# Moving a reciprocal, weight copies, biases and an attention-output projection within the seventh attention step, and interleaving the last four output tiles

## The reference

```python
x = _layernorm(x + _L0_attn_ref(x, w_qkv, b_qkv, w_out, b_out))
x = _layernorm(x + _L0_ffn_ref(x, up_weight, down_weight, up_scale, down_scale, output_scale))
# attn: softmax(q k^T / sqrt(32) + causal) v, then @ w_out.T + b_out
# ffn:  relu((x @ sign(up).T) * up_scale) @ sign(down).T * down_scale * output_scale
```

## Time and profile before

| what | value |
|---|---|
| median of 3 runs | 760.01 us (758.69 to 762.78) |
| the profiled execution | 762.44 us |
| its span in the trace | 760.7 us |
| PE busy | 717.5 us (94%) |
| PEld, DVE, POOL, ACT busy | 68%, 55%, 52%, 43% |
| mean granted TensorE clock | 0.983 of full speed |

### The profile page before, as it was taken

The page is one execution under the profiler, slowest core; times in us unless marked ns, Lnnn a source line. Parts: engine busy times, 40 slices in busy tenths (PEclk is TensorE's granted clock), DMA queues, the critical chain, the costliest instruction groups (busy, mean ns, idle before and its releaser), DMA issues.

```text
span 760.7 us, 11957 instructions
## 1 busy us (share of the span) xinstructions
PE 717.5 (94%) x4112; PEld 515.3 (68%) x4112; DVE 419.7 (55%) x1024; ACT 324.3 (43%) x647; POOL 392.1 (52%) x527
## 2 busy tenths in 40 slices
PE   6899999999999999999798889999999999999993
PEld 4688666666676666665453657678888787878882
DVE  4176485674857657476378441384683359324515
ACT  5211365665655566555345386532321222222210
POOL 4561467493864839657259328662352235223333
PEclk9999999999999999999889999999999999999997
DMA  6975464636455362563727364515005001000101
GB/s 235 297 214 168 103 186 135 177 83 176 147 155 162 93 176 88 155 181 99 188 90 235 97 211 142 164 44 153 16 15 152 28 1 56 1 1 14 43 0 56
DMA packets 47797, 90.02 MB, mean 118 GB/s; under 512 B 5821, under 2 KB 14781, under 8 KB 47609
## 3 DMA queue, kind: packets, MB, share of 16 engines
q1 hardware_dynamic: 38712, 84.02, 37.2%
q10 hardware_dynamic: 9024, 5.24, 2.3%
HBM read 59.38 MB, written 29.61 MB: 117 GB/s over the span
## 4 chain that ended last, share of the span: by engine, by line
PE 79%; DVE 6%; POOL 5%; issue 4%; DMA 4%; ACT 2%; SPq 1%; DVEq 0%; POOLq 0%; ACTq 0%
PE ps_proj L1096 10%; PE ps_heads L1197 8%; PE ps_proj L1248 7%; PE ps_unit L1248 6%; PE ps_score L1273 6%; PE ps_unit L1132 6%; PE ps_unit L1219 5%; PE ps_unit L1164 5%; PE ps_sum L1191 4%; PE ps_score L1164 4%; PE ps_score L1132 3%; PE ps_sum L1273 2%; PE ps_heads L1273 2%; PE ps_unit L1273 2%; PE ps_score L1116 1%
## 5 line engine op out<-in xcount | busy, mean ns | idle before, releaser
L780 POOL TENSOR_TENSOR hid_low<-hid_raw,hid_high 128x512 fp32r<-128x512 f32 (+1 forms) x80 | 90.0, 1126 | 168.2 <-DVE hid_high L1031 167.0
L837 ACT ACTIVATE probs<-ps_unit 128x512 f32<-128x512 f32 (+3 forms) x214 | 101.8, 490 | 88.8 <-PE ps_unit L1164 84.5
L837 ACT ACTIVATE probs<-ps_score 128x512 f32<-128x512 f32 (+3 forms) x170 | 82.4, 495 | 80.0 <-PE ps_score L1164 77.0
L743 POOL TENSOR_SCALAR_AFFINE_SELECT probs<-probs 128x128 f32<-128x128 f32 x256 | 75.9, 315 | 73.5 <-ACT probs L837 70.0
L943 DVE CUSTOM_DVE_ANT_0 ps_unit<-ps_unit,causal 128x128 f32<-128x128 f32 (+3 forms) x162 | 80.6, 513 | 48.4 <-PE ps_unit L1132 47.5
L1031 DVE CAST hid_high<-hid_raw 128x512 fp32r<-128x512 f32 (+1 forms) x80 | 34.1, 426 | 126.9 <-ACT hid_raw L900 126.3
L1132 PE MATMUL ps_unit<-stack 96*128 96x512 f32 (+3 forms) x242 | 84.4, 360 | 8.5 <-DVE maxes L943 5.5
L756 POOL TENSOR_TENSOR added<-added,probs 128x512 f32<-128x512 f32 x64 | 82.4, 1298 | 0.0
L1197 PE MATMUL ps_heads<-probs,v_rows 128*32 128x512 f32 (+3 forms) x768 | 81.0, 504 | 0.0
L1164 PE MATMUL ps_unit<-stack 98*128 98x512 f32 (+2 forms) x214 | 77.0, 363 | 0.1
L737 POOL TENSOR_TENSOR parts<-qk_full,parts 128x512 fp32r<-128x512 f32 x32 | 41.3, 1290 | 56.7 <-ACT parts L816 56.7
(11 more groups left out here) (216 smaller groups left out, 1469.9 us busy)
## 6 DMA issues: line engine op xcount, KB each, us to landing
stack<-qk_parts SPq DMA_DIRECT2D x96, 256.0 KB, 4.6
qk_parts<-parts SPq DMA_DIRECT2D x32, 512.0 KB, 2.9
v_all<-h_even ACTq DMA_DIRECT2D x16, 256.0 KB, 3.6
v_rows<-v_all SPq DMA_DIRECT2D x8, 512.0 KB, 4.2
heads_t<-heads_sb SPq DMA_DIRECT2D x16, 256.0 KB, 2.6
x_tile<-x_rows SPq DMA_DIRECT2D x16, 256.0 KB, 5.3
raw<-up_w SPq DMA_DIRECT2D x8, 512.0 KB, 3.6
raw<-down_w SPq DMA_DIRECT2D x8, 512.0 KB, 3.6
```

What stands on the lines that cost most here:

```text
L743: nc.gpsimd.affine_select(out=tile, in_=tile, compare_op=ALU.is_ge, fill=0.0, base=0, pattern=[[1, P]], channel_multiplier=-1).then_inc(s_ ...
L780: nc.gpsimd.tensor_tensor(parts2[1][:, (HM * s + n) % 3, 0:tokens(s)], full[:, n % 2, 0:tokens(s)], parts2[0][:, (HM * s + n) % 3, 0:token ...
L837: nc.scalar.activation(probs[:, (NP * s + n) % RING, 0:width], bank(what, s, n)[:, off:off + width], ACT.Exp, scale=SCALE).then_inc(s_exp, 1)
```

## The change

It alters slot numbers in `plan()` and adds one wait on DVE. Nothing is computed that was not computed before.

```diff
-ALONE = [[11.2, 13.5, 15.7, 18.3, 28, 30, 32.2, 36, 39.5, 43, 46.5, 50.3],
+ALONE = [[11.2, 13.5, 15.7, 18.3, 28, 30, 32.2, 36, 40.6, 43.3, 46.5, 50.3],
...
-        put(t + (43.9 if paired else 39.4 - s % 2), "sum_added", s)
+        put(t + (43.9 if paired else (40.5, 38.4)[s % 2]), "sum_added", s)
...
-    signs = [late + 39, late + 41.5] + [late + 44 + 3.3 * k for k in range(14)] + [late + 88.9, late + 91.6]
+    signs = [late + 37.2, late + 39.4] + [late + 44 + 3.3 * k for k in range(14)] + [late + 88.9, late + 91.6]
...
-        put(at + (2.9, 5, 3)[k], "invert", k)
-        put(at + (4.4, 6, 4)[k], "scatter", k)
+        put(at + (6.9, 5, 3)[k], "invert", k)
+        put(at + (8.5, 6, 4)[k], "scatter", k)
...
-        put(late + 40 + 1.3 * i, "bias", 0, i)
+        put(late + 44.5 + 1.5 * i, "bias", 0, i)
         for m in range(12):
-            put((late + 45, late + 47.6, last + 1.7, last + 4.5)[i] + 0.22 * m, "attn", 0, 12 * i + m)
-        put((late + 47.5, last + 2.3, last + 4.6, last + 7.4)[i], "y", 0, i)
+            put((late + 45.6, late + 48.2, last + 2.4, last + 5)[i] + 0.22 * m, "attn", 0, 12 * i + m)
+        put((late + 48.1, last + 2.9, last + 5.1, last + 7.8)[i], "y", 0, i)
...
-        put((last + 12.2, last + 12.7, last + 14, last + 14.5)[i], "turn", 0, i)
+        put((last + 13.2, last + 13.7, last + 14.8, last + 15.3)[i], "turn", 0, i)
...
-            put(t + m if r else last + 14.8 + 1.95 * m, "up", r, m)
+            put(t + m if r else last + 15.6 + 1.95 * m, "up", r, m)
             if r < len(ROUNDS) - 1 or m < HM - 2:
-                put(t + m + 2.5 if r else last + 19.7 + 1.95 * m, "down", r, m)
+                put(t + m + 2.5 if r else last + 20.5 + 1.95 * m, "down", r, m)
...
         for q in tiles:
-            put(end, "z", i, q)
-            put(end + 1.05 + q, "ln2", i, q)
-            put(end + 1.95 + q, "out", i, q)
+            if r < len(ROUNDS) - 1:
+                put(end, "z", i, q)
+                put(end + 1.05 + q, "ln2", i, q)
+                put(end + 1.95 + q, "out", i, q)
+            else:
+                put(end + (0, 0.1, 0.2, 1.1)[q], "z", i, q)
+                put(end + 1 + q, "ln2", i, q)
+                put(end + (2.5, 3.5, 4.5, 5.5)[q], "out", i, q)
...
                 for m in range(12):
-                    put(t + (5.2 if i else 3) + at, "attn", i + 1, 12 * q + m)
-                put(t + (6 if i else 4.2) + at, "y", i + 1, q)
-                put(t + (6.7 if i else 5.1) + at, "ln1", i + 1, q)
-                put(t + (7.4 if i else 6.4) + at, "turn", i + 1, q)
+                    put(t + (5.2 if i else 4) + at, "attn", i + 1, 12 * q + m)
+                put(t + (6 if i else 5.2) + at, "y", i + 1, q)
+                put(t + (6.7 if i else 6.1) + at, "ln1", i + 1, q)
+                put(t + 7.4 + at, "turn", i + 1, q)
...
                     dve.wait_ge(s_zr, TT * s + n + 1)
+                    wait(dve, s_mom2, TT * s + n)
                     nc.vector.bn_stats(stats[:, 1, :], z_sb[:, n, :]).then_inc(s_bn, 1)
```

## The result

The changed kernel takes 752.33 us (median of 4 runs, 750.92 to 753.71), the one before 760.25 beside it: a ratio of 0.990, 95% interval 0.987 to 0.993, so some 7.9 us or 1.0% are gained where 15.1 were forecast. The profiled execution took 753.71 us, with a span of 751.6; against the 760.7 of before that is 9.1 us less. The times of the two profiled executions, 762.44 and 753.71, lie 2.2 and 1.4 us above their medians, so that part of the difference to 7.9 is between executions and not between kernels.

A forecast was written before the change was run, and what follows sets the result against it. PE was taken to set the pace, with the gain in its waits and half clock from 360 to 450 us. Terms -8.5 - 4.5 - 1.0 + 0.2 - 1.3 = -15.1 us gave 745 us, range 741.5 to 751.

The forecast's parts named there:

- The first reciprocal: Seventh step, DVE: reciprocal moved behind eight maxima removes PE's 4.4 us wait and 4.7 us of half clock; -8.5 us.
- The rival of late sums: Gathered sums land 2 us later, DVE and PE stand again, the clock falls; 751.7 us, chance 0.08.
- `w_out_low`: Before the output matmuls: earlier halves on POOL remove PE's 3.1 us wait and 1.7 us of half clock; -4.5 us.
- I take two thirds of that as hidden: Of 4.7 us that POOL's two halves could add to DVE's work, two thirds vanish in DVE's idle time.
- The rival that came nearest was the second: POOL holds DVE up; PE's wait becomes one for the heads' low parts; term -1.5, 748 us, chance 0.12.
- The third stretch of low clock: PE at clock 0.66 from 393 to 398 us, losing 1.7 us, with no single long wait ahead.
- the first rival: More comes back: low clock at 393 to 398 us and small waits go too; 741.5 to 743 us, chance 0.10.
- The transposes of the first chunk: Transposes one slot later, other PE work filling waits of 1.8 and 0.7 us; -1.0 us, between 0 and -2.5.
- the fourth rival: Slower than before: bare 1.6 us wait ahead of round 2 makes the clock fall and stay down; chance 0.02.
- The second chunk: One slot later: PE's 1.4 us wait goes, a bare wait of 1.6 before round 2 comes; +0.2 us.
- the rival of a slower kernel: New bare wait of 1.6 us ahead of round 2 lowers the clock lastingly; 765 us with 40 us, chance 0.02.
- The last four tiles: End of run, DVE: next tile's statistics run during a tile's square root; -1.3 us, between -0.5 and -1.7.

The follow-up runs named there:

- low_in_pieces: The changed kernel with each of the two `w_out_low` subtractions on POOL cut into four pieces of 128x256; 749.04 us, ratio 0.986 to the kernel before.
- changed_again: The changed kernel, unaltered, measured again in a later group; 750.96 us, ratio 0.989 to the kernel before.
- tail_undone: The changed kernel with the last four tiles' instructions back in the order of before; 753.70 us, ratio 0.990 to the kernel before.
- recip_only: The kernel before with only the first reciprocal and the copy of its result to DRAM four slots later; 754.54 us, ratio 0.992.
- loads_later: The changed kernel with the loads of the first chunk's x tiles and the constants issued later; 751.09 us, ratio 0.987 to the kernel before.

## Why the prediction was wrong by half

*The first reciprocal*, -8.5: right, -8.7. DVE had no idle time ahead of `early_inv`, the clock stayed at 1.00 to 384 us, and the edit alone shows the same stage. It came to the reciprocal at 373.23, forecast 373. The rival of late sums did not come about.

*`w_out_low`*, -4.5: this is the step that failed; it gave -0.6. The wait that it names did go. But the sentence "I take two thirds of that as hidden" was wrong. Of the 4.7 us by which I saw DVE held up, I put the part that counts at a third, on the ground that DVE had idle time. In the changed kernel DVE had hardly any between the first product and the last difference, and its maxima stand between them: every delay of one of these operations is a delay of the next maximum, for which PE's banks wait. I had also bounded the delay by the length of the two `w_out_low`. The 5.7 us went through five POOL instructions and two selects more. They came in two of the six profiles that have the early slots with an uncut `w_out_low`; but the three products and four differences together took 8.0 to 11.4 us in all six, against 6.5 us before and 5.9 to 7.2 us in the four with early slots and pieces. The rival that came nearest was the second: POOL holds DVE. It had the mechanism, not the place (I looked for it in the low parts, it struck a product and PE waited for a maximum), and its price of 3 us was 0.9 us short.

The other half of the term was the 1.7 us of half clock behind the wait, counted as regained. The low clock at 420 us went, but in each of the six profiles with early slots and an uncut `w_out_low` another stood in the same stage: its mean clock there was 0.77 to 0.92, against 0.92 before. PE's idle time in the stage was 5.4 to 5.9 us in four of the six, about the 5.4 of before, and 2.2 us in the other two. With the pieces the stage took 17.79 us in low_in_pieces against 21.68 before, 3.9 us less: 1.6 us less waiting and no low clock. That is near what the term would have been without POOL's hold. That POOL's hold on DVE makes PE wait is shown by the rows and by the cut into pieces; why the clock falls where no long wait stands ahead of it, as in changed_again, stays open.

*The third stretch of low clock* had no term; the first rival had it go. It went in three profiles of the fourteen and stayed in the rest, and the stage it lies in took 16.5 us without it and 17.6 to 19.4 with it where PE had no wait for the stack. The two waits ahead of it, 0.7 and 0.5 us, are the same in all fourteen profiles. In the changed kernel's profile it cost 1.4 us more than before, twice (changed_again). No edit here was aimed at it, and why it varies between executions stays open; it alone makes 3 us of difference between profiles of the same program up to there (16.56 us in tail_undone, 19.40 in changed_again).

*The transposes of the first chunk*, -1.0: -0.7, and 59.8 to 60.0 us in all twelve profiles with it. Without it the stage took 60.5 us before and 62.1 in recip_only, where the clock fell behind the 1.8 us wait that the shift removes; so it is worth 0.7 or some 2.2 us, as that fall comes or not. The argument under the fourth rival that no fall stood behind a wait of 1.8 us holds for the one profile that I had.

*The second chunk*, +0.2: +1.2. The new wait came where it was foreseen, 1.4 us, named by `t_odd_low`. The mis-sized part is mainly the old one: I had the 1.4 us wait for `x_tile` gone, and 0.8 of it are left; some 0.4 us more are in no wait that the rows name. No clock fell behind the new wait, so the rival of a slower kernel had nothing to stand on.

*The last four tiles*, -1.3: -1.56, with the last norm waiting for the second tile's store as foreseen:

```profile
748.49 0.55 DVE L1068 TENSOR_SCALAR out_sb<-z_sb,mom,rstd 128x512 f32<-128x512 f32 x1 [0.64 <-DMA out<-out_sb]
```

By these terms: -0.2 - 8.7 + 1.4 - 0.6 - 0.7 + 1.2 - 1.6 = -9.2, and the spans differ by 9.1. Of the 6 us missing from the forecast 15.1, `w_out_low` has 3.9, the third stretch 1.4 and the second chunk 1.0; the other terms came out 0.4 us better. By the medians 7.2 us are missing. (The chances given for a faster kernel add up to 0.97, not 0.96.)

## What to carry to other kernels

Where a long subtraction or addition of SBUF tensors is moved on POOL, list what DVE does with two SBUF operands in the same stretch and what is queued behind it; idle time of DVE elsewhere hides nothing. If the two can't be kept apart, try POOL's instruction in pieces: it then took 3.7 and 4.1 us instead of 2.3, and the kernel was still some 2 us faster; at the late slots the pieces brought nothing and may have cost 2 us, so this has to be measured in place. A stall removed early makes every later transfer that was issued by the same queue relatively later, so look at which load lands next (here the reciprocals and `w_out`), before moving one ahead of another that PE needs.

## What the runs showed that I had not expected

DVE does not always get its turn when POOL's current instruction ends. Beside additions and selects of POOL in an unbroken row, the product got in after the first addition (changed_again, loads_later), after a select (before, 406.11 to 407.54), or only when POOL had nothing more to do (5.71 and 5.70 us), and the two that waited longest stood 0.6 us into POOL's addition just as the short ones did. A select of 128x128, with one SBUF operand, takes part in this too: one was stretched from 0.29 to 0.75 us while a product ran. Which side wins at such a boundary is not settled by these runs.
